# Exchanged source halves in the odd chunks of a state-space layer's scores, with four smaller edits, on one core

## The reference

```
proj = u @ W_in.T                       # x, B, C, z and the log decays
xBC  = causal depthwise conv, 4 taps
Lm   = exp(segsum(-softplus(A_log)))    # lower triangle, 512 x 512 a head
M    = einsum('blhn,bshn,bhls->bhls', Cm, Bm, Lm)
y    = einsum('bhls,bshp->blhp', M, x) + D * x
out  = y * silu(z + z_bias) @ W_out.T
```

## Time and profile before

| quantity | value |
|---|---|
| median of 3 runs | 574.33 us |
| the profiled execution's own time | 574.32 us |
| its span, first to last instruction | 572.5 us |
| mean granted TensorE clock | 0.994 |
| PE busy, share of the span | 98% |
| DVE busy | 83% |
| ACT busy | 68% |
| POOL busy | 36% |

### The profile page before, as it was taken

How to read it: one execution, slowest core, us unless ns; L and a number is a source line. 1 busy time by engine, 2 the same in 40 slices (tenths; PEclk the granted TensorE clock), 3 DMA queues, 4 the chain that set the end, 5 groups by cost and what they waited for, 6 DMA issues and landing times.

```text
span 572.5 us, 18109 instructions
## 1 busy us (share of the span) xinstructions
PE 562.0 (98%) x6696; PEld 452.1 (79%) x6696; DVE 473.6 (83%) x753; ACT 387.3 (68%) x960; POOL 207.3 (36%) x377
## 2 busy tenths in 40 slices
PE   7999999999999999999999999999999999999997
PEld 4577787787877778777877878787688988989887
DVE  6899999899899989988999999999767648647343
ACT  1789888888788788877888887888534233323240
POOL 4852464563564464786246234426000000000000
PEclk8899999999999999999999999999999999999999
DMA  8644453433433436433343346446433043100101
GB/s 269 259 148 162 135 191 125 149 127 128 151 110 122 160 107 196 165 110 110 129 148 109 123 168 179 154 142 192 145 97 106 1 123 98 38 2 0 38 0 38
DMA packets 39660, 70.93 MB, mean 124 GB/s; under 512 B 4548, under 2 KB 10948, under 8 KB 39368
## 3 DMA queue, kind: packets, MB, share of 16 engines
q1 hardware_dynamic: 39624, 70.47, 37.4%
HBM read 57.34 MB, written 13.12 MB: 123 GB/s over the span
## 4 chain that ended last, share of the span: by engine, by line
PE 87%; DVE 8%; issue 1%; DMA 1%; POOL 1%; ACT 1%; SPq 0%; DVEq 0%; POOLq 0%; ACTq 0%
PE ps L337 18%; PE ps L339 18%; PE ps L338 18%; PE ps L506 11%; PE ps L489 5%; PE ps L550 5%; PE ps L541 4%; PE ps L525 4%; DVE acc L1015 3%; PE ps L616 2%; DVE acc L1103 2%; DMA u_sb<-in_u 1%; PE ps L562 1%; PE ps L626 1%; PE ps L426 1%
## 5 line engine op out<-in xcount | busy, mean ns | idle before, releaser
L1103 DVE SCALAR_TENSOR_TENSOR acc<-ps,cw_dve,acc 128x511 f32<-128x511 f32 (+2 forms) x384 | 259.1, 740 | 1.8 <-ACT acc L783 0.3
L815 ACT ACTIVATE decay<-sums,p_slot 128x128 f32<-128x128 f32 x512 | 160.7, 397 | 0.8
L1381 POOL TENSOR_SCALAR_AFFINE_SELECT sums<-sums 128x512 f32<-128x512 f32 x128 | 82.4, 646 | 174.4 <-DMA sums<-running_sums 169.6
L783 ACT ACTIVATE acc<-ps,cw_act 128x512 f32<-128x512 f32 x128 | 93.1, 776 | 46.7 <-PE ps L550 44.5
L337 PE MATMUL ps<-ht_hi,wg_hi 128*128 128x512 f32 x256 | 106.9, 418 | 1.6 <-POOL wg_lo L1314 1.0
L339 PE MATMUL ps<-ht_hi,wg_lo 128*128 128x512 f32 x256 | 101.1, 395 | 0.0
L338 PE MATMUL ps<-ht_lo,wg_hi 128*128 128x512 f32 x256 | 101.0, 394 | 0.0
L1091 DVE TENSOR_TENSOR mix<-ps,decay 128x1024 f32<-128x1024 f32 x64 | 78.0, 1219 | 20.5 <-PE ps L506 19.3
L930 ACT ACTIVATE silu_sb<-ps 128x512 f32<-128x512 f32 x32 | 19.2, 599 | 77.4 <-PE ps L339 77.4
L506 PE MATMUL ps<-acc 64*64 64x64 f32 (+1 forms) x2048 | 69.8, 255 | 0.2 <-DVE acc L1103 0.2
L506 PEld LDWEIGHTS ps<-acc 64*64 64x64 f32 x2048 | 54.4, 132 | 9.1 <-issue 8.4
(11 more groups left out here) (136 smaller groups left out, 900.3 us busy)
## 6 DMA issues: line engine op xcount, KB each, us to landing
sums<-running_sums SPq DMA_DIRECT2D x128, 256.0 KB, 3.2
y_parts<-yt_sb SPq DMA_DIRECT2D x32, 256.0 KB, 2.0
wg_raw<-in_w_bc SPq DMA_DIRECT2D x8, 512.0 KB, 4.6
stage<-y_parts SPq DMA_DIRECT2D x16, 256.0 KB, 4.2
u_sb<-in_u SPq DMA_DIRECT2D x4, 512.0 KB, 4.4
stage<-in_w SPq DMA_DIRECT2D x1, 2048.0 KB, 13.3
x_channels<-acc SPq DMA_DIRECT2D x8, 256.0 KB, 2.3
ee<-decay_rows SPq DMA_DIRECT2D x8, 256.0 KB, 4.2
```

What stands on the lines that cost most here:

```text
L783: af(acc[:, b % 2, t, :], ps[:, PROJ_BANK[t], :], ACT.Identity, bias=cw_act[:, t, 1:2], scale=cw_act[:, t, 0:1]).then_inc(s[f"tap_a{t}"], 1)
L815: i = af(decay[:, j, c * P:(c + 1) * P], sums[:, j, c * P:(c + 1) * P], ACT.Exp, scale=-1.0, bias=p_slot[:, b * CH + c, j:j + 1])
L1103: stt(a[:, d:], ps[:, PROJ_BANK[t], 0:L - d], cw_dve[:, t, TAPS - 1 - d:TAPS - d], a[:, d:], ALU.mult, ALU.add).then_inc(s[f"taps{t}"], 1)
L1381: gp.affine_select(out=v, in_=v, compare_op=ALU.is_ge, fill=FAR, base=0, pattern=[[0, CH], [1, P]], channel_multiplier=-1).then_inc(s["mas ...
```

## The change

There are five edits.

1. `scores` writes source half `h` to output partitions `64 * (1 - h)` in the odd chunks 1 and 3. Everything indexed by the source position in those chunks is exchanged too: `p_transposes` makes the exchanged columns with two matmuls against the identity for each odd chunk, `mask` becomes two instructions (the second on 64 partitions, 2 x 128 elements), and `own_x` becomes two copies, of which the odd one reads `x_swapped`. That tile is filled by eight DMAs in group 0 (`swap_halves`) and has the memory of `gates`, whose load moves behind the last step and waits for the last `own_x`.
2. DVE's last tap of tile 2 stands before `mix_pair(q, 1)`.
3. `cw_dve` is copied in two parts, for tiles 2 and 3 in `b = 0` before the first mix, for tiles 0 and 1 in `b = 3` after it.
4. The high parts of tiles 1 and 0 of the next group are made by ACT, in the steps with `b = 3` after `last_tap` of tile 0. POOL keeps the low parts and tiles 3 and 2.
5. ACT's loop ends a group earlier, and the last group's four steps are written out.

```diff
@@ sync
+            def swap_halves(b):
+                sp.wait_ge(s["xtok_ev"], 2 * (b + 1))
+                odd = x_tok[:, b * CH + 1:(b + 1) * CH:2, :]
+                for h in range(2):
+                    sp.dma_start(x_swapped[NS * (1 - h):NS * (2 - h), b], odd[NS * h:NS * (h + 1)]).then_inc(s[f"ld_xs{b}"], 16)
...
             step(0, 2, 0)
-            sp.wait_ge(s["st_gates"], 16)
-            for b in range(B):
-                sp.dma_start(gates[:, b]...)
...
             step(NG - 1, B - 1, NG - 1)
+            sp.wait_ge(s["st_gates"], 16)
+            sp.wait_ge(s["xs_done"], 2 * NG * B)
+            for b in range(B):
+                sp.dma_start(gates[:, b]...)
             sp.wait_ge(s["proj2"], NG * B)
             load(u2[:], u_b[0], "ld_res")
@@ tensor
+                            at = h if c % 2 == 0 else 1 - h
-                            i = mm(ps[NS * h:NS * (h + 1), 2 + a, c * P + NS * h:(c + 1) * P],
+                            i = mm(ps[NS * at:NS * (at + 1), 2 + a, c * P + NS * h:(c + 1) * P],
@@ scalar
                 last_tap(g, b, 0)
+                if split:
+                    act.wait_ge(s["ld_wg"], (g + 2) * 16)
+                    nc.scalar.copy(wg_hi[:, 1], wg_raw[:, 1]).then_inc(s["w_high_act"], 1)
+                    nc.scalar.copy(wg_hi[:, 0], wg_raw[:, 0]).then_inc(s["w_high_act"], 1)
@@ vector
                 tap(g, b, 3, 2)
+                tap(g, b, 2, 2)
                 mix_pair(q, 1, first)
-                tap(g, b, 2, 2)
@@ gpsimd
+                gp.tensor_copy(xs[:, b % 2, 0::2, :, 0:HD], even...).then_inc(s["xs_done"], 1)
+                gp.tensor_copy(xs[:, b % 2, 1::2, :, 0:HD], odd...).then_inc(s["xs_done"], 1)
...
-                v = sums[:, j, :].rearrange("p (c l) -> p c l", c=CH)
-                gp.affine_select(out=v, in_=v, ..., base=0, pattern=[[0, CH], [1, P]],
+                v = sums[:, j, :].rearrange("p (c e l) -> p c e l", c=2, e=2)
+                gp.affine_select(out=v, in_=v, ..., base=0, pattern=[[0, 2], [NS, 2], [1, P]],
                                  channel_multiplier=-1).then_inc(s["masked"], 1)
+                await_unit("masked", 8 * n + 2 * j + 1)
+                o = v[0:NS, :, 1, :]
+                gp.affine_select(out=o, in_=o, ..., base=-NS, pattern=[[0, 2], [1, P]],
+                                 channel_multiplier=-1).then_inc(s["masked"], 1)
```

More of the change, by code:

```diff
@@ L142, in adaln_ssm_ffn_kernel @@
         h2_lo = sb("h2_lo", [P, KT, L], F32R)
+        x_swapped = gates
         zeros = sums[:, 2, 0:L // 2].bitcast(BF16)
@@ L258, in _ @@
                 load_sum(0, 0, j, first=True)
+            swap_halves(0)
             store_x(2)
@@ L261, in _ @@
             load_group(1)
+            swap_halves(1)
             step(0, 1, None)
@@ L410, in p_transposes @@
                 for c in range(CH):
-                    i = nc.tensor.transpose(ps[:, 7, c * P:(c + 1) * P], sums_t[:, c * P:(c + 1) * P], ident)
+                    if c % 2 == 0:
+                        nc.tensor.transpose(ps[:, 7, c * P:(c + 1) * P], sums_t[:, c * P:(c + 1) * P], ident)
+                    else:
+                        for h in range(2):
+                            i = mm(ps[NS * (1 - h):NS * (2 - h), 7, c * P:(c + 1) * P],
+                                   sums_t[:, c * P + NS * h:c * P + NS * (h + 1)], ident, start=True, stop=True)
                 i.then_inc(s["ptok_mm"], 1)
@@ L897, in _ @@
             for b in range(2, B):
-                step(0, b, gq=0, gr=0)
-            with act.Fori(1, NG) as g:
+                step(0, b, gq=0, gr=0, split=(b == B - 1))
+            with act.Fori(1, NG - 1) as g:
                 for b in range(B):
-                    step(g, b, gq=(g - 1 if b == 0 else g), gr=(g - 1 if b < 2 else g))
+                    step(g, b, gq=(g - 1 if b == 0 else g), gr=(g - 1 if b < 2 else g), split=(b == B - 1))
+            for b in range(B):
+                step(NG - 1, b, gq=(NG - 2 if b == 0 else NG - 1), gr=(NG - 2 if b < 2 else NG - 1))
             last, r = NG * B - 1, NG * B - 2
@@ L1146, in step @@
                 tap(g, b, 0, 2)
+                if b == 0:
+                    dve.wait_ge(s["taps2"], g * (3 * B))
+                    nc.vector.tensor_copy(cw_dve[:, 2:4], conv_sb[:, bass.ds(g * GT + 2, 2), 0:3]).then_inc(s["cwd_late"], 1)
                 mix_pair(q, 0, first)
+                if b == B - 1 and not front:
+                    dve.wait_ge(s["taps0"], g * (3 * B) + 3 * B)
+                    nc.vector.tensor_copy(cw_dve[:, 0:2], conv_sb[:, bass.ds(g * GT + GT, 2), 0:3]).then_inc(s["cwd"], 1)
                 if front:
                     y_own(0, 1)
+                if b == 0:
+                    dve.wait_ge(s["cwd_late"], g)
                 tap(g, b, 3, 0)
@@ L1309, in split_tile @@
             def split_tile(g, t):
-                n = (g * GT + PLACE[t]) * 2
-                gp.tensor_copy(wg_hi[:, t], wg_raw[:, t]).then_inc(s["w_split"], 1)
-                await_unit("w_split", n + 1)
+                if not (isinstance(g, int) and g == 0) and t < 2:
+                    await_unit("w_high_act", g * 2 + PLACE[t] - 1)
+                else:
+                    gp.tensor_copy(wg_hi[:, t], wg_raw[:, t]).then_inc(s["w_high"], 1)
+                    await_unit("w_high", g * 2 + PLACE[t] + 1)
                 gp.tensor_tensor(wg_lo[:, t], wg_raw[:, t], wg_hi[:, t].bitcast(F32), ALU.subtract).then_inc(s["w_split"], 1)
```

37 lines of the change are left out of this document (21 added, 16 removed).

## The result

The changed kernel takes 577.62 us (median of 6 runs, 573.62 to 579.94), the kernel before in the same comparison 574.08 (573.59 to 575.11). The ratio is 1.0053, with a 95% interval of 1.0032 to 1.0074: slower by half a per cent, small but clear of no change. The forecast was 564.1 us, its range ended at 570.5, and slower had a chance of 0.10.

The account below looks back on a forecast made before the run. The prediction took PE to bound the kernel, busy 98% of the span. It summed 574.3 - 12.9 (scores) + 0.6 (stall at 258 us) + 1.4 (last step) + 0.7 (late gates) = 564.1 us; eight times in ten 561.5 to 570.5.

Parts of the forecast that it names:

- the scores: PE's score matmul groups: each falls from 1.02 to 0.82 us, 63 groups on the chain, 12.9 us off.
- Rival 3: PE's score matmuls: program order holds, narrow ones can't run ahead, and it gets slower, 578.2 us; chance 0.06.
- Rival 1: Steps: DVE or ACT takes over at 10.85 us a step, total 570.4 us; chance 0.12.
- It hides behind POOL's waits for DMAs: POOL's added masks and `own_x` copies: covered by its DMA waits of 5.2 us a step, except where cover is missing.
- Rival 2: POOL's work and the late loads: their costs are larger than forecast, total 568.1 us; chance 0.10.
- The stall at 258 us: PE's 1.01 us wait for POOL's low part behind the butterflies: grows by 0.6 us (0 to 1).
- The last step: POOL's queue ahead of `y_add`: DVE's gate multiply, `out_project` and all behind come 1.4 us later (0.5 to 2.2).
- DVE's edits (2, 3): DVE's moved tap and split coefficient copy: nothing added but a small copy, gain and cost 0.
- Does the shorter group meet a wait?: PE behind the shorter scores: `states` keeps 0.24 us, DVE 0.2 us of waiting; the 0.41 us a step fits.
- Gates after `own_x`: Gate and `u2` loads after the last `own_x`: DVE's add comes late, cost +0.7 us (0 to 2).
- High parts on ACT: ACT's two casts, at most 1.0 us in one step of four: covered by its wait for `intra`, price 0.
- `p_transposes`: Start-up, four short matmuls instead of two transposes: below 0.2 us beside DVE's taps, cost 0; +0.2 if open.

Follow-up runs that it names:

- e12: e9 with the load of `u2` ahead of the gates' and batch 1's rows held until the first residual half is done; 562.40 us.
- e1: The kernel before with only the exchange of output halves in the odd chunks' score matmuls; 568.45 us.
- e7: The changed kernel with the last tap of tile 2 behind the second mix again; 579.01 us.
- e8: The kernel before with the scores' exchange and the last tap of tile 2 ahead of the second mix, nothing else; 566.22 us.
- e2: The changed kernel with the one mask instruction a row of the kernel before; 567.99 us.
- e3: The changed kernel with POOL's butterflies spread one a step over six steps, instead of two a step over three; 572.03 us.
- e4: The changed kernel with POOL's last step reordered, both scalings and both additions of y and `own_x` ahead of the masks that stood before them; 575.05 us.
- e11: The changed kernel with POOL's last step reordered, POOL also waiting for DVE's products before its adds and for the gate multiplies before its masks; 573.37 us.
- e5: The changed kernel with DVE's two coefficient copies moved to ACT and ACT's `p_slot` copy behind the copies of the states; 572.21 us.
- e10: The changed kernel with `own_x` reading `x_tok` in odd chunks too, no `swap_halves`, and the gates loaded early; 575.83 us.
- e9: e6 with POOL's last step as in e11, and `load_rows(0)` and `load_y(0, 0)` one step later; 565.76 us.
- e6: The changed kernel with e5, e3 and e4 together, and `p_transposes` behind `x_project(3, 1)` and `x_transposes(1, 0)` in the start-up; 566.85 us.

## Why the prediction was wrong

**Right: the scores.** The price of a narrow matmul, the four quarters side by side and the narrow ones running ahead gave 0.82 us a group; it is 0.81. A step is 10.68 us and not the forecast 10.62: before it was 11.06 and not 320.00 / 29 = 11.03, since fewer than 29 steps lie in that stretch, and 0.38 us come off it, not 0.41. The term of -12.9 becomes 31 x -0.38 = -11.8. e12 comes out 12.0 us below before, but 1.2 us of that is the stall at 258 us, which it no longer has. In the price of a narrow matmul there was luck: `states` has weights of 64 columns, but its matmuls are 24, 16 or 8 wide, not 64. The rows of `scores` itself would have been the ones to take it from. Rival 3, by which narrow ones can't run ahead, is out, and with it the rule of strict program order (the Trainium skill, TensorE: Matmul & The Clock Gate, Part 3, The mechanism): by it the group couldn't have become shorter. Rival 1 is out as well, but only by edit 2: with the old place of the tap a plain step is 10.82 us (e1, e7), close to its 10.85. In e12 DVE is busy 308.22 of 320 us, and the plain steps are at 10.68.

**Wrong: what the long queue on POOL costs.** It is three steps of the prediction, and one that isn't there.

The three go back to one sentence, *"It hides behind POOL's waits for DMAs"*: on the mean of a step it does, and in the steps that matter those waits aren't there. Rival 2 had these costs larger, but its total was 568.1.

1. *"The stall at 258 us. ... Cost +0.6 (0 to 1)."* The wait grew from 1.01 to 2.4 us, 0.8 more than said. I balanced one cast against one half mask. The faster PE alone makes it 1.9 (e8), the cast on ACT brings it down to 1.2 (e2, which has no second masks), and the second masks add 1.2. For POOL had worked without a gap since 239.5, so that five second masks, at 0.40 + 0.22 = 0.62 us where I took 0.45, stood ahead of the low part, partly in the place of a wait for a DMA of 2.3 us that POOL had before. e3, which takes butterflies out of the way, and e2, without second masks, both remove the excess.
2. *"The last step. ... come 1.4 us later"*. PE's wait is 3.7 us; with 0.5 and 1.4 it would be 1.9. The second masks in the queue were counted rightly, four, but at too low a price: with the wait before each they take 0.62, 0.93, 1.19 and 0.81 us, 3.55 together, where I had 0.2 and three times 0.45. That DVE isn't free beside POOL costs 0.4 us here (1.10 for 0.69); it decides only once the queue is put in another order, as e4 and e11 show.
3. *"DVE's edits (2, 3). Nothing is added but a small copy. ... Gain and cost 0."* The copy, held beside POOL's longer queue, costs about 1.7 us: +0.66, +0.56 and +0.49 in three steps. The moved tap, which I also put at 0, is worth 0.14 us a step, and without it the faster PE would have gained over a third less a step (10.82 against 10.68 from 11.06, e1 and e8).
4. *No step: the clock.* I priced each wait of PE at its own length. The granted clock fell to 0.5 behind the long ones, and 6.8 us there cost about 3 us more, at two places (PE's busy time is 13.95 us in the one step, and 10.68 in a plain one; 16.13 in the other, and 13.13 in e11). This is the largest single term. Of six runs of the changed kernel the one whose mean clock was 0.994, as before's, took 573.62 us; the others, at 0.981 to 0.990, took 576.58 to 579.94.

**Wrong, small: "Does the shorter group meet a wait? ... Nothing is late."** I looked at `states` and its copy of `b_tok`, but not at the transposes behind `scores`, which want ACT's copy of the states. In the steps with `p_slot` ahead of it that copy is 0.25 us late, seven times: 1.8 us. This has nothing to do with POOL's queue, since e8 has the same seven steps. e5 removes it.

**Gates after `own_x`, +0.7.** Hidden in the changed kernel, because PE and DVE were later for POOL's sake (e10); seen as soon as POOL was less late: DVE waits 1.19 and 1.56 us for gates and `u2` in e2, 1.77 and 1.58 in e11, 2.60 and 1.76 in e9. The mechanism was right, its place in the sum wasn't.

**High parts on ACT, `swap_halves`, `p_transposes`.** No loss was found in the first two, and in the step of unit 18 the cast on ACT helps (1.9 us of waiting in e8, 1.2 in e2). The first scores stand 1.5 us later than before, but in the other kernels with the same start-up they stand between 56.4 and 57.6 us; how much of it is `p_transposes` stays open.

The account, on the profiled execution (578.5 against 564.1, 14.4): clock 3.3 + 3.0, the middle wait 0.8, PE's last wait 1.8, long steps 3.9, size of the scores' term 1.1, start-up 1.5, the rest -0.4, and -0.7 for the gates that did not show. That is 14.3. The first 3.3 is an upper value: up to 0.5 us of it also stands behind a wait without a drop (PE busy 11.19 in e5's step, 10.68 in a plain one).

What stays open: no run separates the clock's fall from the wait ahead of it by will. In all profiles each fall between the first scores and the end of the mixer stands behind a long wait of PE, and e3, which removes the wait at 258 us, removes the fall. But the length of the wait doesn't settle it. No drop followed waits of 1.0 to 1.2 us (before, e2's middle, e12), 1.5 (e1), 1.9 (e8) and 2.3 (e5). Drops of 3.4 us followed waits of 1.4 (e2), 1.9 (e11), 2.1 (e9), 2.3 (e10, e11), 2.6 (e4) and 3.7 (e5). Drops of 6.8 us followed 2.0 (e7), 2.4 (the changed kernel), 2.7 (e6), 3.3 (e3) and 3.7 (the changed kernel, e10). What decides between them I can't say.

## What to carry to other kernels

When work is moved to an engine that "has room", the average says nothing: find the places where its idle cover (here a wait for DMAs) is missing, count its whole queue back to its last pause, and price the instruction and the wait between two that depend on each other. Then ask of every engine that is to become faster who waits behind the shortened piece, and price a PE wait of well over 1 us at up to 3 us above its length. The gain was in the change all the time: what lost it was order on POOL, ACT and the load queue, and that could be mended without taking any work out.

## What was not expected of the hardware

DVE instructions whose inputs all lie in SBUF can be held while POOL runs without a gap: a 128x6 copy 0.21 to 1.96 us, the product 0.74 to 2.13, two gate multiplies 1.29 to 2.71. Taps and mixes, which read PSUM, kept about 0.74 and 1.22 us in the same stretches. It goes the other way too: in the changed kernel DVE's product starts at 390.30 and takes its usual 0.74 us, and POOL's second mask, begun at 390.35, takes 0.96 us and not 0.40. The Trainium skill (SBUF — State Buffer, SBUF: two separate sides) has the rule: DVE with two SBUF inputs, or in a fast two-port mode, and GpSimd share one pair of ports, and whoever starts first keeps it for its whole instruction. The traces agree, and show how it adds up: a DVE instruction can be held for more than one of POOL's. e4's product starts at 387.33, beside an addition that ends at 387.97, and itself ends at 389.46, behind two copies and a mask.
